# Expert blocks in units of two, three and three, and four pieces of work put in another order

## The reference

```
x = x + linear_attention(layernorm(x))          # 16 heads, relu features, causal
x = x + cross_attention(layernorm(x), context)  # 77 keys, masked softmax
x = x + ffn(layernorm(x))

ffn:  shared = LN(silu(x@sw1) * (x@sw2)) @ sw3               # all 4096 tokens
      x_moe  = x[index_b, index_t]                           # 512 chosen tokens
      expert = argmax(sigmoid(x_moe@eg_w) + exp_bias)        # one of 8
      w      = softmax(shared gate score, expert score)      # two weights
      e_out  = LN(silu(x_moe@ew1[expert]) * (x_moe@ew2[expert])) @ ew3[expert]
      ffn at a chosen token = w[0]*shared + w[1]*e_out
```

## Time and profile before

| | |
|---|---|
| median of 3 runs | 379.18 us (378.64 to 379.2) |
| the profiled execution | 378.86 us, its span 377.1 us |
| granted TensorE clock | 0.998 |
| PE busy | 360.6 us, 96% |
| DVE busy | 296.2 us, 79% |
| POOL busy | 279.4 us, 74% |
| ACT busy | 162.8 us, 43% |
| DMA | 34.51 MB, mean 92 GB/s |

### The profile page before, as it was taken

The page is one execution under the profiler, slowest core; times in us unless marked ns, Lnnn a source line. Parts: engine busy times, 40 slices in busy tenths (PEclk is TensorE's granted clock), DMA queues, the critical chain, the costliest instruction groups (busy, mean ns, idle before and its releaser), DMA issues. The chain is left out here.

```text
span 377.1 us, 10708 instructions
## 1 busy us (share of the span) xinstructions
PE 360.6 (96%) x3531; PEld 257.0 (68%) x3534; DVE 296.2 (79%) x922; ACT 162.8 (43%) x394; POOL 279.4 (74%) x414
## 2 busy tenths in 40 slices
PE   8999999999999999999999999999999999998992
PEld 4565777777777777767777777777766656655551
DVE  2588788988998899898989878887666678799762
ACT  1553453463455355445434623533456444422220
POOL 5337988776677876777876788888978889668555
PEclk9999999999999999999999999999999999999999
DMA  7994781300300120031221013004000232239760
GB/s 240 328 306 103 227 261 28 74 16 16 65 23 30 28 61 16 17 72 61 95 41 46 17 23 80 16 17 85 16 30 15 73 111 71 98 116 284 231 201 25
DMA packets 39310, 34.51 MB, mean 92 GB/s; under 512 B 4505, under 2 KB 38456, under 8 KB 39256
## 3 DMA queue, kind: packets, MB, share of 16 engines
q1 hardware_dynamic: 36392, 29.54, 27.6%
q0 software_dynamic: 1312, 3.37, 2.9%
q10 hardware_dynamic: 1552, 0.92, 0.8%
HBM read 17.55 MB, written 12.60 MB: 80 GB/s over the span
## 5 line engine op out<-in xcount | busy, mean ns | idle before, releaser
L1668 POOL TENSOR_TENSOR s_t<-s_t,causal 128x512 f32<-128x512 f32 x63 | 78.9, 1272 | 15.6 <-ACT s_t L978 15.4
L539 PE MATMUL bank<-h1t,w_qkv 128*128 128x512 f32 x112 | 52.9, 595 | 0.4 <-DVE x L1237 0.3
L1224 DVE TENSOR_TENSOR s_t<-sbank,causal 128x512 f32<-128x512 f32 x65 | 43.5, 671 | 1.1 <-PE sbank L560 1.0
L1660 POOL TENSOR_TENSOR state_wide<-state,own_pair 128x256 f32<-128x256 f32 x28 | 18.9, 675 | 25.5 <-DVE state L1215 24.4
L978 ACT ACTIVATE s_t<-sbank 128x512 f32<-128x512 f32 x63 | 33.7, 587 | 7.8 <-PE sbank L560 7.8
L560 PE MATMUL sbank<-arena 32*128 32x256 f32 x512 | 36.7, 400 | 0.0
L599 PE MATMUL bank<-s_t,vp 128*32 128x128 f32 x1024 | 34.6, 275 | 1.1 <-DVE s_t L1224 0.4
L546 PE MATMUL bank<-w_qkv,h1t 128*128 128x256 f32 x128 | 34.2, 389 | 0.0
L1676 POOL TENSOR_TENSOR rr<-ve,neg_half 128x3 f32<-128x3 f32 x36 | 31.9, 887 | 3.0
L684 PE MATMUL bank<-w_out,attn_t 128*128 128x256 f32 x128 | 33.6, 385 | 0.5 <-DVE attn_t L1305 0.5
L778 PE MATMUL sbank<-h1t,w 128*128 128x512 f32 x72 | 33.0, 596 | 0.5 <-ACT h1t L978 0.5
(11 more groups left out here) (233 smaller groups left out, 836.1 us busy)
## 6 DMA issues: line engine op xcount, KB each, us to landing
rden_t<-rden SPq DMA_DIRECT2D x64, 64.0 KB
rows<-x SPq DMA_DIRECT2D x32, 128.0 KB, 1.9
x<-in_x SPq DMA_DIRECT2D x7, 512.0 KB, 8.0
out<-x SPq DMA_DIRECT2D x7, 512.0 KB
we<-in_we SPq DMA_DIRECT2D x1, 2048.0 KB
xmask<-in_mask POOLq DMA_DIRECT2D x2, 616.0 KB, 10.2
rows<-empty SPq DMA_DIRECT2D x1, 1032.0 KB, 4.9
we<-in_we SPq DMA_DIRECT2D x1, 1024.0 KB
```

What stands on the lines that cost most here:

```text
L539: mm = pe.matmul(dst[:, :], w_qkv[:, ch, cb * P:(cb + 1) * P], h1t[:, g % 3, ch, :], start=(ch == 0), stop=(ch == CH - 1))
L1224: dve.tensor_tensor(s_t[:, r, :, :], sbank[r][:, :].rearrange("p (s q) -> p s q", s=4), causal[:, :].unsqueeze(1).to_broadcast([P, 4, P]), ...
L1668: pool.tensor_tensor(s_t[:, r, :, :], s_t[:, r, :, :], causal[:, :].unsqueeze(1).to_broadcast([P, 4, P]), ALU.mult)\
```

## The change

Expert units become M0 with blocks 0 and 1, M1 with blocks 2 to 4, and M2 with blocks 5 to 7. Four orders change: `invert_variance(1)` stands behind the first gather, not the second; `scale_gathered` stands at the head of ACT's round q = 5; `add_gate_bias` stands ahead of `y_evict(4)`; the stores of F7 stand ahead of `load_base(0)` in SP's queue.

```diff
-UB = 3
-NMG = -(-NBLK // UB)
+FIRST_OF = (0, 2, 5, NBLK)
+NMG = len(FIRST_OF) - 1
...
         def blocks_of(k):
-            return range(UB * k, min(UB * k + UB, NBLK))
+            return range(FIRST_OF[k], FIRST_OF[k + 1])
...  (SP)
+                if what == "F":
+                    store_out(k)
                 if n == FIRST_M - 1:
                     load_base(0)
-                if what == "F":
-                    store_out(k)
...  (PE, y_products)
                     if is_moe(n) and j % 2 == 0:
-                        wait(pe, ys_ready, UB * UNITS[n][1] - max(0, UB - 2 - j))
+                        wait(pe, ys_ready, FIRST_OF[UNITS[n][1]] - (max(0, size(n - 1) - 2 - j) if UNITS[n][1] else 0))
...  (ACT)
             for q in range(3, NU + 1):
+                if q == GATHERED - 1:
+                    scale_gathered()
                 gates(q, 0)
...
-                if q == GATHERED - 1:
-                    scale_gathered()
...  (DVE)
+                if q == GATHERED:
+                    add_gate_bias()
                 if q != FIRST_M:
                     y_evict(q - 2, 2 if q == FIRST_M + 1 else 0, 2 if FIRST_M + 2 <= q <= NU else GT)
                 if q == GATHERED:
-                    add_gate_bias()
                     choose_experts()
...  (POOL)
                 gather(m, g_x2, rows, idx_u, gathered)
-                if m == 1:
+                if m == 0:
                     invert_variance(1)
```

More of the change, by code:

```diff
@@ L762, in to_features @@
                         else:
-                            src = hs_in[:, UB * k + j, ch * P:(ch + 1) * P]
+                            src = hs_in[:, FIRST_OF[k] + j, ch * P:(ch + 1) * P]
                         mm = transpose(sbank[ch][:, j * P:(j + 1) * P], src)
@@ L789, in gate_products @@
                     for j in range(own.start, own.stop):
-                        b = UB * k + j
+                        b = FIRST_OF[k] + j
                         dst = sbank[2 + half][:, (j - own.start) * D:(j - own.start + 1) * D]
@@ L824, in z_features @@
                         for j in range(lo, hi):
-                            wait(pe, mzn_ready, UB * k + j + 1)
+                            wait(pe, mzn_ready, FIRST_OF[k] + j + 1)
                             mm = transpose(bank[part_bank(n, lo)][:, j * P:(j + 1) * P], m_z[:, j, :])
@@ L850, in y_products @@
                     else:
-                        b = UB * UNITS[n][1] + j
+                        b = FIRST_OF[UNITS[n][1]] + j
                         wait(pe, mzt_ready, UNITS[n][1] + 1 + (j >= parts(n)[0][1]))
@@ L1394, in gated @@
                         wait(dve, mztr_done, k)
-                        wait(dve, mzn_ready, UB * k)
+                        wait(dve, mzn_ready, FIRST_OF[k])
                         dve.scalar_tensor_tensor(out=m_z[:, own, :], in0=x12[:, :, 1, :], scalar=0.5,
@@ L1399, in gated @@
                         wait(dve, mz_ready, 2 * k + (j >= rows_of(n, 1).start) + 1)
-                        wait(dve, mzmv_ready, UB * k)
+                        wait(dve, mzmv_ready, FIRST_OF[k])
                         dve.bn_stats(g_zstats[:, j, :], m_z[:, j, :]).then_inc(mstat_done, 1)
```

## The result

| | before | changed |
|---|---|---|
| median of 6 runs each | 379.19 us (378.64 to 379.69) | 382.70 us (381.85 to 382.89) |
| ratio | | 1.0095, interval 1.0079 to 1.0111 |
| profiled execution, its span | 378.86, 377.1 | 382.51, 380.7 |
| mean granted clock | 0.998 | 0.992 |

What follows compares the result with a forecast made beforehand. The prediction took chains of waits, not PE's 96% busy time, as the bound. Last scatter -0.65 and base +0.2 gave -0.45: span 376.65, forecast 378.7 us against the median, range 378.2 to 379.2, with rivals 377.8 to 380.0.

Steps and rivals of the forecast that it cites:

- The odd weights: PE before M1: five blocks' weights land 351.6, wanted 352.8, 1.2 us slack; rival late by 1: 379.5 us, chance 0.06.
- The base: DVE's eviction of M0: the base lands at 359.3, wanted at 358.4; cost 0.25, taken as 0.2 us.
- the base late: Rival, M0's base: scatters held by F7's stores, load lands 360.5; 379.9, or 380.9 with stores' 1 us; chance 0.14.
- Two, three, three: Expert units up to the end: M2's last scatter starts at 373.15 against 373.80, 0.65 us earlier.
- The power: POOL, power behind the first gather: a wait of POOL goes, F3's eviction 0.8 us earlier, at 316.7.
- ACT's scaling: Ahead of PE's transposes of unit G: scaling first saves PE some 0.45 us, logits end near 322.6.
- The bias: DVE, bias ahead of F4's eviction: choice begins 1.2 us earlier, 0.75 from the eviction, 0.45 from the round trip to ACT.
- the front gains less: Rival, ahead of the experts: DVE's or POOL's chain gives only 0.45 us; sum +0.3, 379.5 us, chance 0.10.
- The store: SP's queue, F7's stores ahead of the base: cost nothing by cover of the base's wait, up to 1 us without.
- The sum: Whole kernel: -0.65 for the last scatter + 0.2 for the base = -0.45 us, span 376.65.

Runs made afterwards that it cites:

- own_weights: The changed kernel with a semaphore per unit, so PE waits only for that unit's odd weights; 380.07 us, 1.0039.
- late_stores: The changed kernel with the stores of F5, F6 and F7 all behind load_base(0) in SP's queue; 379.95 us, 1.0051.
- units_only: The kernel before with units of two, three and three and the old four orders; 380.96 us, 1.0073.
- own_drop: own_weights without the stores of F5 and F6, so 1 MB of the output stays unwritten; 378.38 us, 0.9985.
- orders_only: The changed kernel with units of three, three and two again, the four orders kept; 377.92 us, 0.9976.
- own_old_store: own_weights with F7's stores behind load_base(0) again; 380.81 us, 1.005.
- orders_no_store: orders_only with F7's stores behind load_base(0) again; 378.46 us, 0.9985.

## Why the prediction was wrong, step by step

- **The odd weights, the step that failed.** The prediction put PE's want at 352.8, and PE was ready at 352.7. It put the landing at 349.7 + 1.9 = 351.6; the load was issued at 350.07 and took 5.42, to 355.49. The 1.9 is not a landing of weights, nor of any load. It is this row of the page of the kernel before:

```profile
rows<-x SPq DMA_DIRECT2D x32, 128.0 KB, 1.9
```

These are the 32 stores of `x` into `rows`, in the loop over the tiles; they share nothing with the weights but their 128 KB. For the weights the page has no landing time. The load stood in a stretch at 95 to 106% of the DMA engines, with 1.5 MB of stores right behind it. The rival was named, and with it the right place, but its slack of 1.2 us came from the 1.9, its price of 1.0 was for weights late by 1, and the sum booked nothing. Real size: 3.00 of wait, 2.6 of them lost, plus the lower clock.
- **The clock.** No step priced what a wait of PE does to the granted clock. It is 0.8 (traces) to 1.5 (medians) of the 3.5.
- **The base.** Forecast: issue 355.9, cost 0.2. In own_weights, where it is not hidden behind the weights, it was issued at 358.13 and cost 1.61 on DVE. That is the rival "the base late", and late_stores bears out its mechanism, the scatters held by the stores. It named F7's stores only; those of F5 and F6 and the fifth block's weights count as well (units_only, with F7's stores behind, was issued at 358.98), and even own_drop had 1.10 of it. The Trainium skill, "DMA: Bandwidth & Descriptors", section on queues, rings and completion order, would have had the scatters pass by taking turns packet by packet. The traces do not show that as a saving: 5.9 us to landing beside the stores, 2.9 without them.
- **Two, three, three by itself.** From M2's last statistic to the last scatter the forecast had 364.3 to 373.15, 8.85; measured 368.62 (368.32 + 0.30) to 377.46, 8.84. The step was right in its length, and in its parts too (2.75 from the end of the normalization, 370.77, to the last evictions, and 1.37 from there to the scatter), and began 4.3 late. But even with most of the waits gone these units gain nothing: counted from the first gather, own_drop's last scatter is at 74.62, against 74.04 in orders_only, where the last unit has two blocks, and 74.28 in the kernel before.
- **The power.** Forecast 316.7 for F3's eviction, measured 316.63. The mechanism is borne out: POOL has no idle time left there, and without this order the gain at the choice is all but gone (27.04 against 27.08). That the position fits is luck: the trace was 0.40 early at the first gather, and from there the gain is 0.44, not 0.8.
- **ACT's scaling.** Logits forecast at 322.6; the bias, released by them, began at 322.19. Counted from the first gather the logits end 0.59 earlier, where 0.45 was booked. How much of it is this order's stays open, since no experiment took it alone.
- **The bias.** Forecast -1.2 in the choice; measured from the first gather -0.50 at the end of its first instruction, and F4's eviction alone is 0.54 earlier (0.75 was booked). The round trip's 0.45 was there (the instruction started 1.02 earlier) and was lost to POOL's add, which the prediction had not looked at: a step "beneath" another engine's work was booked as if engines did not hold each other. So the rival "the front gains less" came true as well, with 0.50 where it had 0.45; by its own sum that alone would have cost 0.3, not 3.5.
- **The store.** Booked at nothing, bound 1 us. The runs don't tell it from nothing: own_weights and own_old_store differ by 0.7 in its favour by the medians, orders_only and orders_no_store by 0.5, both within their intervals. What matters more is that 1.5 MB of stores and the weights share the stretch.
- **The sum.** The forecast had the last scatter 0.65 earlier (373.15), and gave 0.2 of that back for the base. Counted from the first gather it came 4.06 later. Own weights take 2.46 of this away (75.88), the 1 MB of stores a further 1.26 (74.62), and 0.34 are left. The clock's share lies within the first of these terms, so it is not added to them.

Not one of the kernels with two, three, three was faster than the orders alone in units of three, three and two. Open: why a load ahead of stores in its queue lands later for them, and why the scatters do. The runs show both with the stores there and away; they don't show which part of the path is shared. Own weights together with late stores were not tried.

## What to carry to other kernels

When a change makes an engine want a buffer earlier, take the landing from the DMA of that very stretch, with what is queued right behind it, and look up which transfer a landing time on the page belongs to. If the page has none for yours, the slack is unknown. Also give each consumer its own semaphore before reordering units. A gain ahead of a transfer that does not move is no gain, and may cost more than itself where the longer wait lowers PE's clock. Work "beneath" another engine has to be looked up in that engine's timeline as well: here an add of 2.35 us on POOL held short instructions of DVE until it ended. And before a gain of tenths is read off two traces, count both from a row ahead of everything that was changed.

## What the runs showed of the hardware

- A 128 KB load of weights took 5.42 us to land with 1.5 MB of stores right behind it in its queue, 5.00 with 1 MB, some 3.5 with 0.5 MB, and about 3.8 with none; the base's last scatter in the other queue was followed by the load that waits for it after 5.9 us with all the stores and 2.9 without.
- PE idle for 3.00 us behind four dummies of 1.03 us: granted clock 0.80, 0.50, 0.84 in the three windows of 2 us behind it (356 to 362). Idle for 2.13 us in units_only: 1.00 throughout. With sixteen dummies in the wait (fill_wait): 1.00 from 350 to 365.
- A DVE tensor_scalar (0.18) and a DVE tensor_tensor (0.19), both within SBUF, last until 0.04 to 0.05 us behind the end of a POOL tensor_tensor of 2.35 us beside them (0.70, 2.04); a reciprocal (0.38) and an eviction of products out of PSUM (1.66 for four) do not. The Trainium skill, "GPSIMD Engine Reference", section 1 on specifications, states that POOL shares its interfaces to SBUF with DVE and that DVE instructions in a two-port mode or with two SBUF inputs contend. The traces agree for the tensor_tensor, and show the contention as a hold to the end of POOL's instruction (2.04 us for one of 0.19), not as a slowing; in which mode the tensor_scalar ran they don't show.
